# Chunked recurrence of a two-layer block: sixteen heads in one pass against two halves of eight, with another loading order

## The reference, cut to what matters

```python
def step(S, inp):                       # 64 chunks, one after the other
    qi, ki, vi, ei = inp
    kh = einsum('bchd,bhde->bche', ki, S)
    target = vi - ki
    mu = mean(kh, -1); rstd = rsqrt(var(kh, -1) + EPS)
    kh_hat = (kh - mu) * rstd
    g = w * kh_hat + b - target
    gw = g * w
    v_new = (gw - mean(gw, -1) - kh_hat * mean(gw * kh_hat, -1)) * rstd
    A = einsum('bchd,bshd->bhcs', qi, ki)
    A = where(tri, A, 0) * ei
    qh = einsum('bchd,bhde->bche', qi, S) - einsum('bhcs,bshe->bche', A, v_new)
    S = S - einsum('bchd,bche->bhde', ki * ei[..., None], v_new)
    return (S, qi + _ln(qh, w, b))
```

## Time and profile before

| what | us |
|---|---|
| median of 3 runs | 2606.64 |
| lowest, highest | 2590.48, 2607.16 |
| the profiled execution's own time | 2608.55 |
| its span, first to last instruction | 2606.8 |
| the recurrence's first instruction, and the end of its last result copy (start 1156.30) | 768.4, 1156.6 |
| mean granted TensorE clock over the span | 0.899 |

### The profile page before, as it was taken

How to read it: one execution, slowest core, us unless ns; L and a number is a source line. 1 busy time by engine, 2 the same in 40 slices (tenths; PEclk the granted TensorE clock), 3 DMA queues, 4 the chain that set the end, 5 groups by cost and what they waited for, 6 DMA issues and landing times. The chain is left out here.

```text
span 2606.8 us, 59064 instructions
## 1 busy us (share of the span) xinstructions
PE 2213.7 (85%) x23684; PEld 1917.1 (74%) x23684; DVE 1536.4 (59%) x3549; ACT 1116.8 (43%) x2103; POOL 859.6 (33%) x666
## 2 busy tenths in 40 slices
PE   7999992999967999975679985999999999999920
PEld 6777772777747898963447765999998999999920
DVE  4545543566636877749947424565665566566658
ACT  4334432466652322224421113555555555555523
POOL 0000000122220000006300775665665566666621
PEclk9999995999987877758989997999999999999965
DMA  2110103355556646324320003423246524324147
GB/s 108 39 39 31 36 31 121 122 209 201 202 214 126 160 115 157 92 55 170 133 87 1 1 1 112 141 77 138 73 143 234 179 68 143 115 98 138 35 185 281
DMA packets 154572, 300.44 MB, mean 115 GB/s; under 512 B 67097, under 2 KB 93209, under 8 KB 139645
## 3 DMA queue, kind: packets, MB, share of 16 engines
q1 hardware_dynamic: 108285, 181.71, 21.8%
q0 software_dynamic: 44480, 115.41, 13.2%
q10 hardware_dynamic: 1616, 0.62, 0.1%
HBM read 296.72 MB, written 106.27 MB: 155 GB/s over the span
## 5 line engine op out<-in xcount | busy, mean ns | idle before, releaser
L91 PE MATMUL bank<-routed_xh,routed_guh 128*128 128x256 f32 (+1 forms) x1536 | 438.7, 286 | 27.4 <-DVE routed_xl L2173 27.4
L92 PE MATMUL bank<-routed_xh,routed_gul 128*128 128x256 f32 (+1 forms) x1536 | 438.5, 285 | 0.0
L93 PE MATMUL bank<-routed_xl,routed_guh 128*128 128x256 f32 (+1 forms) x1536 | 436.4, 284 | 0.0
L2207 DVE TENSOR_TENSOR routed_gul<-routed_guf,routed_guh 128x2816 fp32r<-128x2816 f32 x64 | 198.0, 3094 | 251.1 <-ACT routed_guh L2150 251.1
L91 PEld LDWEIGHTS bank<-routed_xh,routed_guh 128*128 128x128 f32 (+1 forms) x1536 | 282.0, 184 | 34.3 <-issue 31.6
L2091 POOL DMA_INDIRECT routed_x<-mid_x,routed_xi x132 | 273.2, 2069 | 55.5 <-issue 53.0
L92 PEld LDWEIGHTS bank<-routed_xh,routed_gul 128*128 128x128 f32 (+1 forms) x1536 | 281.7, 183 | 2.1
L93 PEld LDWEIGHTS bank<-routed_xl,routed_guh 128*128 128x128 f32 (+1 forms) x1536 | 283.3, 184 | 0.0
L2100 POOL DMA_INDIRECT mid_y<-routed_y,routed_yi x132 | 138.9, 1052 | 248.7 <-ACT routed_y L2166 226.1
L2160 ACT CAST routed_ih<-routed_sil 128x256 fp32r<-128x256 f32 (+1 forms) x192 | 78.0, 406 | 242.4 <-DVE routed_sil L2212 242.4
L2150 ACT CAST routed_guh<-routed_guf 128x2816 fp32r<-128x2816 f32 x64 | 163.5, 2555 | 33.4 <-DMA routed_guf<-in_GU,routed_wi 28.8
(11 more groups left out here) (456 smaller groups left out, 5690.9 us busy)
## 6 DMA issues: line engine op xcount, KB each, us to landing
last_y<-mid_y SPq DMA_DIRECT2D x16, 1536.0 KB, 9.7
mid_ks<-ffn_kT SPq DMA_DIRECT2D x16, 1024.0 KB
mid_qs<-ffn_qT SPq DMA_DIRECT2D x16, 1024.0 KB
ttt_KQ<-mid_ks SPq DMA_DIRECT2D x16, 1024.0 KB, 7.0
ttt_KQ<-mid_qs SPq DMA_DIRECT2D x16, 1024.0 KB, 12.5
mid_te<-ffn_te SPq DMA_DIRECT2D x16, 264.0 KB, 4.1
ttt_te<-mid_te SPq DMA_DIRECT2D x64, 66.0 KB, 6.5
gla_xT<-in_xT SPq DMA_DIRECT2D x16, 256.0 KB, 3.2
```

Of the source, the lines that this page charges most:

```text
L91: pe.matmul(out, hi(c), whi(c), start=start and c == 0, stop=False, skip_group_check=True)
L92: pe.matmul(out, lo(c), whi(c), start=False, stop=False, skip_group_check=True)
L93: last = pe.matmul(out, hi(c), wlo(c), start=False, stop=stop and c == n - 1, skip_group_check=True)
L2207: nc.vector.tensor_tensor(gul[q][:].rearrange("p a c n -> p (a c n)"), guf[q][:], guh[q][:].bitcast(F32).rearrange("p a c n -> p (a c n)") ...
```

## The change

1. The 16 heads are cut into two halves of eight (h = 0, 1; two of the four groups each, GH = 2). Every semaphore of the ring exists per half, the banks bS, bQ, bH, bA too; cross is formed from a part of the bQ bank. The elementwise tiles are 128 x 64, the state and cross copies 128 x 128, ub and am 128 x 128 per half. All products of a step are still made, each half's group by itself.
2. DVE's list interleaves the second part of one half with the first part of the other (both). A step has 30 DVE instructions instead of 16, of half the columns, without ub.
3. ub is computed by POOL (by_sequence), after u of the half.
4. Tile 0: the first two steps of KQ (1 MB in all) are issued by ACT, te and the other six steps of KQ by SP, kk by POOL after DVE has cleared the buffer (before, POOL cleared it). te and kk have semaphores of their own, so L1312's counterpart waits for te alone, and the state update for kk. In every later tile te is issued first, then KQ, then kk.
5. "Unread" products: float32r products of zeros into bank columns that nobody reads (or adding zeros): 3 + 20 of 128 x 512 ahead of the first data, 12 of 128 x 512 after the first data and te have landed, 22 of 128 x 384 ahead of the wait for u(0,0) and 6 ahead of that for u(0,1).

The core of the diff:

```diff
+            def load_goals(i):
+                ...
+                for b in range(B):
+                    ...
+                    for j in range(HG):
+                        sp.dma_start(te[f][of_head(b, j)]..., goal_src[j]).then_inc(in_te[f], 16)
             def load(i):
...
+                load_goals(i)
+                load_steps(i, slice(0, ST), in_KQ[f])
                 sp.wait_ge(cleared[f], 1)
...
+                        sp.dma_start(*keys_of_head(i, b, j)).then_inc(in_kk[f], 16)
-            load(0)
+            load_goals(0)
+            load_steps(0, slice(FIRST, ST), in_KQ[0])
             load(1)
@@ gpsimd
             nc.gpsimd.memset(zero[:], 0.0).then_inc(s["zero"], 1)
-            nc.gpsimd.memset(kk[0][:], 0.0).then_inc(cleared[0], 1)
+            pool.wait_ge(cleared[0], 1)
+            for b in range(B):
+                for j in range(HG):
+                    pool.dma_start(*keys_of_head(0, b, j)).then_inc(s["keys0"], 16)
             nc.gpsimd.memset(kk[1][:], 0.0).then_inc(cleared[1], 1)
+            def by_sequence(n, h):
+                pool.wait_ge(done["u"][h], n + 1)
+                nc.gpsimd.tensor_tensor(ub[n % 2][:, heads(h)], u[n % 2][:, heads(h)]..., seq..., ALU.mult).then_inc(done["ub"][h], 1)
@@ scalar
+            for k in range(2):
+                for b in range(B):
+                    act.dma_start(*steps_of(0, k, b, slice(0, FIRST))).then_inc(s["first"], 16)
...
+            for n in range(STEPS):
+                for h in range(HALVES):
+                    if n + 1 < STEPS:
+                        deviation(n + 1, h)     # square, square root
+                        state(n + 1, h)
+                    result(n, h)
+                    if n + 2 < STEPS:
+                        next_keys(n + 1, h)     # cross
@@ vector
+            nc.vector.memset(kk[0][:], 0.0).then_inc(cleared[0], 1)
+            dve.wait_ge(s["zero"], 1)
+            nc.vector.tensor_copy(still[:], zero[:]).then_inc(s["still"], 1)
...
+            def both(n, h, m, k):
+                to_goal(n, h)
+                rates(n, h)
+                along_keys(n, h)
+                masked(n, h)
+                along_summed(n, h)
+                if m < STEPS:
+                    squares_summed(m, k)
+                projected(n, h)
+                if m < STEPS:
+                    weighted(m, k)
+                taken_off(n, h)
+                if m < STEPS:
+                    weighted_summed(m, k)
+                update(n, h)
+                if m < STEPS:
+                    weighted_centred(m, k)
+                    inverse(m, k)
+                    keys_normed(m, k)
+                    weighted_normed(m, k)
+            first_of(0, 0)
             for n in range(STEPS):
...
+                both(n, 0, n, 1)
+                both(n, 1, n + 1, 0)
@@ tensor
+            def unread(out, width, n):
+                for _ in range(n):
+                    pe.matmul(out[:, D - width:], still[:, 0:P], still[:, 0:width], start=False, stop=False, skip_group_check=True)
+            pe.wait_ge(s["still"], 1)
+            for h in range(HALVES):
+                pe.matmul(bS[h][:], still[:, 0:P], still[:], start=True, ...).then_inc(s["s0"], 1)
+            pe.matmul(bA[0][:], still[:, 0:P], still[:], start=True, ...)
+            unread(bA[0], D, 20)
+            pe.wait_ge(s["first"], 16 * 4)
+            pe.wait_ge(in_te[0], 16 * 8)
+            unread(bA[0], D, 12)
+            for h in range(HALVES):
+                keys_times_state(0, h)
+                pe.matmul(bH[h][:, 0:GH * DH], zero..., start=False, stop=True, ...).then_inc(done["KH"][h], 1)
+                prepare(0, h)
+            keys_times_state(1, 0)
+            queries_times_state(0, 0)
             for n in range(STEPS):
...
+                for h in range(HALVES):
+                    if n == 0:
+                        unread(bS[1], D - GH * B * DH, 22 if h == 0 else 6)
+                    pe.wait_ge(done["u"][h], n + 1)
+                    if n + 1 < STEPS:
+                        keys_corrected(n + 1, h)
+                        state_updated(n, h)
+                    queries_corrected(n, h)
+                    m, k = n + h, 1 - h
+                    if m + 1 < STEPS:
+                        keys_times_state(m + 1, k)
+                    if m < STEPS:
+                        queries_times_state(m, k)
+                    if n + 1 < STEPS:
+                        prepare(n + 1, h)
```

More of the change, by code:

```diff
@@ L1356, in keys_times, with of, column, keys_times_state @@
-            def keys_times(out, n, other, made):
-                for g in range(G):
+            def of(h):
+                return range(h * GH, (h + 1) * GH)
+            def column(g, width):
+                return slice(g % GH * width, (g % GH + 1) * width)
+            def keys_times_state(n, h):
+                pe.wait_ge(done["S"][h], max(n, 1))
+                if n:
+                    pe.wait_ge(done["hat"][h], n)
+                for g in of(h):
+                    for b in range(B):
+                        last = pe.matmul(bH[h][half(b), column(g, DH)], keys(n, g, b), S[:, g, b, :],
+                                         start=(g == h * GH), stop=False, skip_group_check=True)
+                last.then_inc(done["KS"][h], 1)
@@ new lines, in queries_times_state @@
+            def queries_times_state(n, h):
+                if n + 1 < STEPS:
+                    pe.wait_ge(done["cross"][h], n + 1)
+                else:
+                    pe.wait_ge(done["qh"][h], n)
+                for g in of(h):
+                    for b in range(B):
+                        last = pe.matmul(bQ[h][half(b), column(g, DH)], queries(n, g, b), S[:, g, b, :],
+                                         start=(g == h * GH), stop=False, skip_group_check=True)
+                last.then_inc(done["QS"][h], 1)
@@ L1358, in keys_times @@
+            def keys_times(out, n, h, other, made):
+                for g in of(h):
                     for b in range(B):
-                        last = pe.matmul(out[half(b), g * R64:(g + 1) * R64], keys(n, g, b), other(g, b),
+                        last = pe.matmul(out[half(b), column(g, R64)], keys(n, g, b), other(g, b),
                                          start=True, stop=True, skip_group_check=True)
-                last.then_inc(s[made], 1)
-            def prepare(n):
-                keys_times(bA, n, lambda g, b: queries(n, g, b), "A")
+                last.then_inc(done[made][h], 1)
@@ L1365, in prepare @@
+            def prepare(n, h):
                 if n + 1 < STEPS:
[L1366 to L1373 removed]
@@ new lines, in prepare, with keys_corrected @@
+                keys_times(bA[h], n, h, lambda g, b: queries(n, g, b), "A")
+            def keys_corrected(n, h):
+                pe.wait_ge(done["cross"][h], n)
+                for g in of(h):
+                    for b in range(B):
+                        last = pe.matmul(bH[h][half(b), column(g, DH)], cross[half(b), g, :], u[(n - 1) % 2][half(b), g, :],
+                                         start=False, stop=True, skip_group_check=True)
+                last.then_inc(done["KH"][h], 1)
@@ new lines, in queries_corrected @@
+            def queries_corrected(n, h):
+                pe.wait_ge(done["am"][h], n + 1)
+                for g in of(h):
+                    for b in range(B):
+                        last = pe.matmul(bQ[h][half(b), column(g, DH)], am[half(b), g, :], u[n % 2][half(b), g, :],
+                                         start=False, stop=(g == (h + 1) * GH - 1), skip_group_check=True)
+                last.then_inc(done["AU"][h], 1)
+            def unread(out, width, n):
+                for _ in range(n):
+                    pe.matmul(out[:, D - width:], still[:, 0:P], still[:, 0:width], start=False, stop=False, skip_group_check=True)
```

295 lines of the change are left out of this document (154 added, 141 removed).

## The result

The changed kernel takes 2751.23 us (median of 4 runs, 2720.28 to 2769.95), the kernel before, run beside it, 2606.9 (2590.48 to 2607.97). The ratio is 1.052, 95% interval 1.046 to 1.058: slower by 144 us where 72 us of gain were forecast, and beyond the range. The profiled execution is the one of 2720.28, the fastest of the four. (Ratios here compare undisturbed executions alone, so that one can differ a little from that of the medians beside it.)

A forecast was written before the change was run, and what follows sets the result against it. Bound by a ring of waits at full clock and PE alone at half clock; steps -64, start -7, tail -1 sum to -72 us from the median of 2606.64, giving 2535 us, range 2515 to 2560.

The forecast's parts named there:

- the one named as deciding: In the recurrence, the halves keep full clock once reached; 63 steps at 4.65 instead of 5.66 us give -64 us.
- the thin part of the step: Idle, small 64x64 products of L1390, state update and L1401 in one piece; blamed for the clock's falls, with 0.61 us idle.
- rival (a): In the recurrence, the clock falls once and stays down, since the halves cut the dense run; at worst 2712 us; chance 0.27.
- Full clock step: A recurrence step in halves at full clock: 4.65 us against 4.88 before, a near tie of DVE and PE.
- Half clock step: A recurrence step in halves at half clock: stays 7.44 us, PE's products being the same in number and shape.
- Start: Tile 0's loads and first u: 10 us earlier on time, -3 if kk is late; -7 us taken.
- Tail and later tiles: After the last u: -1 us; loads of later tiles, issued a tile ahead, hidden: 37 us against 24.6.

The follow-up runs named there:

- before_fill: The kernel before with four unread 128x256 products in each step, ahead of L1390's wait for u; 2592.86 us, ratio 0.997.
- stop4: The changed kernel with one VectorE memset of 3072 columns ahead of the list of step 4; 2763.19 and 2760.71 us, ratio 1.058.
- no_unread: The changed kernel without any unread product, at the start or in the first step; 2763.47 us, ratio 1.059.
- burst_tile: The changed kernel with ten more unread 128x384 products at the start of each of tiles 1 to 7; 2640.06 us, ratio 1.009.
- few_loads: burst_tile with the loads of keys, goals and steps of tiles 2 to 7 cut to a sliver, leaving out needed data; 2655.79 us, ratio 0.994.
- swap: The changed kernel with the queries' correction ahead of the state update in each half; 2738.25 us, ratio 1.050.
- few_keys: burst_tile with only the keys of tiles 2 to 7 cut to 4 of 64 blocks, leaving out needed data; 2647.33 us, ratio 0.995.
- pace_burst: burst_tile with the kk loads of tiles 1 to 7 spread over the steps of the tile before; 2635.14 us against 2609.24.
- swap_burst: burst_tile with the queries' corrections ahead of the state update in each half; 2676.0 us against 2671.84, ratio 0.995.

## Why the prediction was wrong, step by step

The step that failed is the one named as deciding: "So I expect full clock to be kept once it is there". It rested on one cause, the thin part of the step, "although PE mostly idled no more than that 0.61". That cause is real, and the halves did remove it: before_fill loses the short falls, and the changed kernel has none in 57 us, where the one before has one every 10 to 20. But "mostly" hid the second cause, single longer gaps. The earlier trace rows was one, though the clock happened to stay up behind it, and I let it stand in rival (a) as a mere possible trigger. stop4 shows what a single one can do. What the change took away is the recovery: with 16 products of L1492 in a piece instead of 32 of L1359, the clock didn't come back in 395 us (no_unread: 500). That is rival (a) as it was written, with its mechanism. Its chance of 0.27 was too low, because I asked whether a fall would come and not how often: the stretch of the earlier trace rows at 0.50 is one of four that last 20 us and more within 63 steps. Three of these four lie behind a longer wait for u, which the halves take away, and one behind a stop of PE with no reason shown, which they don't. One such stop and no way back is enough: full clock "once it is there" ended in step 13. That it is the cut of the dense run in particular that removes the recovery isn't shown by a run of its own: burst_tile shows that dense products bring it back, not that L1359's 32 did.

Terms of the sum, each against its measurement:
- *Full clock step*: 4.65 forecast, 4.75 measured, by PE, not VectorE. PE's half turn is 2.37, inside the 2.14 to 2.4 that the text gave; I took the middle of a tie. VectorE's 64-column instructions took 0.21 to 0.22 (forecast 0.225), spaced 0.13 to 0.14 when independent, and POOL's ub 0.40 (forecast 0.44). Where the clock holds, as in few_loads, the term would thus have been 63 x (4.75 - 5.66) = -57 instead of -64.
- *Half clock step*: "so a step stays 7.44" failed: it is 8.17. "The same in number and shape" was true of the products, but not of their order. Twelve groups with their changes of shape replace six; swap took back 0.28 of the 0.73, and the rest is open. This is why rival (a) was priced at 2712 at worst and the median lies at 2751: 63 x 0.73 = 46 us on top would make its worst case 2758.
- *Start*: first u 9.8 us earlier, forecast 10 "on time"; but I costed the unread products of step 0 as lying beside VectorE's work (3.8 us, measured 4.09). They began only when PE had finished prepare, at 797.14, and ended 2.9 us after u was ready. I also left out the wait for the 3 MB in step 0 (2.02). With both, 3.4 are left at step 1; I took 7.
- *Tail and later tiles*: the loads were on time, as forecast. What I didn't look for is that they slow another queue, the one that brings instructions. The Trainium skill, page "Runtime: NRT & Kernel Launch", section "Instruction fetch mechanics", says that each engine's instructions come in 16 KiB blocks by a DMA queue of their own while it executes, mostly hidden. The traces agree on the blocks (in few_loads 42 packets of 16 KB for PE's 10,568 weight loads and products of 250 us), and disagree on hidden: beside full loads PE stopped for 1.06 us here and for 1.33 and 1.64 in burst_tile, and with the loads cut away not at all.

The Trainium skill, page "TensorE: Matmul & The Clock Gate", table "Why this matters for your kernels", would have the clock kept without long idle gaps. The measurement decides otherwise here: it fell after a stop of 1.06 us, and before the change 13 times with PE idle no longer than 0.62 us at a time, and it stayed at 0.50 with PE busy 395.00 of 395.00.

## What to carry to other kernels

When the clock falls and returns within a stage, find both causes before a change: what stopped PE ahead of each fall, and which products ran ahead of each return, since a change that splits the densest run can remove the return. Price a rival by how often its trigger is in the trace, and not by whether it might come. Where groups of products of different shape are cut in two, count the changes of shape at either clock, even if no product is added.

## What the runs showed of the hardware that was not expected

- TensorE can be busy without a gap for 500 us and stay at 1.2 GHz, where the same products run for 313 us at 2.4 GHz if the clock was up before and nothing stops them (no_unread, few_loads).
- Ten 128x384 products (2.7 to 3.6 us begun at half clock, 2.0 at full) brought it back in each tile of the profiled executions in which it was down (burst_tile, few_keys, pace_burst, swap_burst). Six (2.29 us) did so in some runs (the changed kernel, stop4, burst_tile, few_loads) and not in others (swap, few_keys, pace_burst, swap_burst).
- A PE that idles 0.61 us in every step of 4.87 (0.83 from start to start) loses the clock for 3.4 us every few steps; with unread products in that gap the falls that are left, three in 324 us, stand behind longer stops (before_fill).
- The 16 KB instruction packets were longer beside full DMA loads, and at full clock PE stopped behind some of the long ones: in few_loads none took over 1.50 from 860 us on and PE never waited; with full loads some took 1.7 to 2.2, with a PE stop behind two of five in burst_tile. At half clock such packets cost nothing: the changed kernel has four of 1.96 to 2.15 between 870 and 1110 us, and no gap.
- A group's start costs more where the shape changes: 0.57 us for eight 64x64 products ahead of a 128x128 one, 0.45 ahead of the same shape, at half clock.
